# Moving two small steps of the key maximum one query product later in a linear-attention stage

## The chip, the cores and the metric

The kernel runs on one core of a Trainium2 chip. The metric is the time of one execution on the device, in microseconds (us), and a kernel's time is the median of its runs. The engines are TensorE (PE in the profile, with PEld for its weight loads), VectorE (DVE), ScalarE (ACT), GpSimd (POOL) and SyncE (SP).

## The reference

A network of two layers over 1024 nodes with 512 features: in each, a graph part, a mixing part and a feed-forward part. The change lies in the mixing part of the first, two blocks (`l` = 0, 1) of attention with random features (8 heads of 64, 256 features each):

```python
def softmax_kernel(data, proj, is_query, eps=0.0001):
    ...
    data_dash = jnp.einsum('bhnd,md->bhnm', data * normalizer, proj)
    diag = jnp.sum(data ** 2, axis=-1, keepdims=True) * 0.5 * normalizer ** 2
    if is_query:
        m = jnp.max(data_dash, axis=-1, keepdims=True)
    else:
        m = jnp.max(data_dash, axis=(-2, -1), keepdims=True)
    ...
    return ratio * (jnp.exp(data_dash - diag - m) + eps)
...
qp = softmax_kernel(q, proj[i], True)
kp = softmax_kernel(k, proj[i], False)
k_sum = kp.sum(axis=2)
d_inv = 1.0 / jnp.einsum('bhnm,bhm->bhn', qp, k_sum)
ctx = jnp.einsum('bhnm,bhnd->bhmd', kp, v)
o = jnp.einsum('bhmd,bhnm,bhn->bhnd', ctx, qp, d_inv)
```

A query row needs only the maximum of its own row before its exponential. The keys need one maximum for a whole head, over all 1024 nodes and 256 features.

## The kernel before, in words

Every engine has a program written out by hand, and semaphores tie them together. Each result of TensorE in PSUM is a job, a bank of 512 columns. There are eight banks; job n takes bank n modulo 8 and waits (`open_job`) until job n-8 has been read. `job_plan` lists the jobs in order, with the engine that frees each: A for ScalarE, D for VectorE. The order of the list must be the order in which TensorE runs them.

The attention of a block works on four pairs of heads (`hp` = 0 to 3), so there are eight pairs in the kernel. Their stretches run from about 140 to 273 us (block 0) and from 567 to 705 us (block 1). A pair goes like this:

- `kd`: eight products of 128 nodes each, keys by random features (L792, two PE instructions for each product). ScalarE copies each to `kd` (L1326), and VectorE then takes its row maxima, `kmax` (L1733).
- For pairs 1 to 3 VectorE then does two subtractions for the output of the pair before (`o_to_lo`, L1726), and after them reduces `kmax` to `kmaxp`, a column of maxima for each of the two heads (L1739).
- `qd`: eight products, queries by random features (L792 too). For each, VectorE takes the negative row maximum (L1743) and adds the diagonal term (L1745); this is the bias `nqmax`, and ScalarE then writes the exponential to `G` (`query_exp`, two instructions on L1334 for each product).
- `kt`: TensorE transposes `kmaxp` (L798), VectorE reduces the two rows to two numbers, `kneg` (L1749), and sets them on a diagonal, `kdiag` (L1751).
- `kb`: TensorE spreads the two numbers to all partitions, `ones` by `kdiag` (L803), and VectorE copies them to `nkmax` (L1755). With `nkmax` as bias ScalarE takes the exponential of the keys in place in `kd`, one instruction for each head (L1341), and counts `kexp_done` after each.
- `ctx`: 64 PE instructions, keys by values (L819). They wait for `kexp_done`: the first half for the first head's exponential, the second half for the second's. It follows the eighth query product on TensorE.
- `eT` turns `G` (L810), `o` multiplies by the context (L833), and VectorE divides.

GpSimd runs beside this: it issues the indirect DMAs that add edges to two tables (L2348), and between them makes the low parts of weights, a pass of about 5 us over 128x2048 elements (`lo`, L2273), when its own list comes to them. In block 1 it has no wait for the attention in its list.

The steps `kt` and `kb` are put inside the loop over the query products: on TensorE after product `t`, on VectorE after the two `nqmax` instructions of product `t`, and on ScalarE the exponentials of the keys come after a number of `query_exp`.

Of the kernel before, what the change touches and what calls it, by code (L numbers as in the profile page):

```python
# [32 lines left out]
D = 512  # L33
NT = N // P
# [65 lines left out]
def job_plan():  # L100

    stages = [("xn_T", 8, "AD"), ("gnn_w_T", 4, "AD"), ("par_T", 1, "D"), ("hg", 4, "A"), ("y_T0", 8, "AD"), ("hg", 4, "A"),
              ("edge_T", 1, "D"), ("proj0", 1, "A")]
    for l in range(DEPTH):
        if l:
            stages += [(f"q{l}", 2, "A"), (f"y_T{l}", 4, "AD"), (f"q{l}", 6, "A")]
        else:
            stages.append((f"q{l}", 8, "A"))  # L110
        stages += [(f"k{l}", 1, "A"), (f"rq{l}", 2, "A"), (f"k{l}", 2, "A"), (f"dq{l}", 1, "A"), (f"k{l}", 5, "A"),
                   (f"v{l}", 1, "D"), (f"rk{l}", 2, "A"), (f"v{l}", 1, "D"), (f"dk{l}", 1, "A"), (f"v{l}", 6, "D"), (f"vsum{l}", 1, "A")]
        for hp in range(HEADS // 2):
            s = f"{l}.{hp}"
            stages += [("kd" + s, 8, "AD"), ("qd" + s, 2, "A"), ("kt" + s, 1, "D"), ("qd" + s, 2, "A"),
                       ("kb" + s, 1, "D"), ("qd" + s, 4, "A"), ("ctx" + s, 1, "D"), ("eT" + s, 8, "D"),
                       ("o" + s, 4, "D")]
        stages += [(f"wo{l}", 6, "D"), (f"y2_T{l}", 4, "AD"), (f"wo{l}", 2, "D"),
                   (f"up{l}.0", 2, "A"), (f"y2_T{l}", 4, "AD"), (f"up{l}.0", 6, "A"), (f"down{l}.0", 8, "D")]
        for fb in range(1, MLP):  # L120
            stages.append((f"up{l}.{fb}", 8, "A"))
            if fb + 1 < MLP or l + 1 == DEPTH:
                stages.append((f"down{l}.{fb}", 8, "D"))
            else:
                stages += [(f"proj{l + 1}", 1, "A"), (f"down{l}.{fb}", 6, "D"), (f"y_T{l + 1}", 4, "AD"), (f"down{l}.{fb}", 2, "D")]
    stages += [("gnn", 6, "D"), ("xt_T", 4, "AD"), ("gnn", 2, "D"), ("gate_T", 1, "A"), ("xt_T", 4, "AD"), ("gate_T", 1, "A"), ("gate", 1, "D"),
               ("deg", 1, "D"), ("rank", 1, "D"),
               ("xT0", visit_tiles(0), "AD")]
    for v in range(VISITS):
        n = visit_tiles(v)  # L130
        stages.append((f"g0.{v}", n, "A"))
        if v:
            stages.append((f"hT{v - 1}", 2 * visit_tiles(v - 1), "AD"))
        stages.append((f"u0.{v}", n, "D"))
        if v:
            stages.append((f"down_e{v - 1}", visit_tiles(v - 1), "A"))
        stages.append((f"g1.{v}", n, "A"))
        if v + 1 < VISITS:
            stages.append((f"xT{v + 1}", visit_tiles(v + 1), "AD"))
        stages.append((f"u1.{v}", n, "D"))  # L140
    stages += [(f"hT{VISITS - 1}", 2 * visit_tiles(VISITS - 1), "AD"), (f"down_e{VISITS - 1}", visit_tiles(VISITS - 1), "A")]
    stages += [("wv_T", 4, "AD"), ("wth_T", 4, "AD"), ("x3_T", 8, "AD"), ("gram", 4, "AD"), ("gwv", 4, "AD"),
               ("kv", 4, "AD"), ("mean", 1, "A"), ("fc_T", 4, "AD"), ("xkv", 8, "D"), ("h", 8, "D"), ("h_T", 4, "AD"),
               ("w0_T", 1, "A"), ("w1_T", 2, "AD"), ("agg0", 2, "D"), ("h_T", 4, "AD")]
    for g in range(2):
        stages += [(f"agg{g}", 8 if g else 6, "D"), (f"f_T{g}", 8, "AD"), (f"rst{g}", 6 if g else 8, "D")]
    stages += [("u_T", 2, "D"), ("rst1", 2, "D")]
    for i in range(STEPS + 2):
        if i == 2:
            stages.append(("u_T", 2, "D"))  # L150
        if i == STEPS:
            stages.append(("alu_T", 1, "D"))
        if i < STEPS:
            stages.append((f"alu_in{i}", 3, "A"))
        if 0 < i <= STEPS:
            stages.append((f"alu_mid{i - 1}", 3, "A"))
        if i > 1:
            stages.append((f"alu_out{i - 2}", 1, "D"))
    stages.append(("alu_T", 1, "D"))
    first, place, seen, who, acts, dones = {}, {}, {}, [], [], []  # L160
    for name, count, engines in stages:
        first.setdefault(name, len(who))
        for _ in range(count):
            place[name, seen.get(name, 0)] = len(who)
            seen[name] = seen.get(name, 0) + 1
            who.append(engines)
            acts.append((acts[-1] if acts else 0) + ("A" in engines))
            dones.append((dones[-1] if dones else 0) + ("D" in engines))
    return first, place, who, acts, dones
# [15 lines left out]
def gps_network(nc, a, out):  # L185
# [67 lines left out]
    with ExitStack() as ctx:  # L253
# [26 lines left out]
        kd = place("kd", [P, 2, NT, NBF], F32, at_b)  # L280
# [342 lines left out]
        def _(pe):  # L623
# [136 lines left out]
            for l in range(DEPTH):  # L760
# [25 lines left out]
                for hp in range(HEADS // 2):  # L786
                    s = f"{l}.{hp}"
                    for x, feat in (("kd", k_T), ("qd", q_T)):
                        for t in range(NT):
                            n = JOB_AT[x + s, t]  # L790
                            open_job(n)
                            pe.matmul(bank(n), feat[:, hp, t * P:(t + 1) * P], proj[:, :, :].rearrange("p a m -> p (a m)"),  # L792
                                      start=True, stop=True).then_inc(job_full, 1)
                            if x == "qd" and t == 1:
                                n = JOB["kt" + s]
                                open_job(n)
                                pe.wait_ge(kmax_ready, 4 * l + hp + 1)
                                pe.transpose(bank(n)[0:2, 0:P], kmaxp[:, :], ident[:, :]).then_inc(job_full, 1)  # L798
                            if x == "qd" and t == 3:
                                n = JOB["kb" + s]  # L800
                                open_job(n)
                                pe.wait_ge(kdiag_ready, 4 * l + hp + 1)
                                pe.matmul(bank(n)[:, 0:2], ones[0:2, :], kdiag[:, :], start=True, stop=True).then_inc(job_full, 1)  # L803
# [365 lines left out]
        def _(act):  # L1169
# [113 lines left out]
            for l in range(DEPTH):  # L1283
# [37 lines left out]
                for hp in range(HEADS // 2):  # L1321
                    s = f"{l}.{hp}"
                    for t in range(NT):
                        n = JOB["kd" + s] + t
                        act.wait_ge(job_full, n + 1)
                        act.activation(kd[:, :, t, :], bank(n).rearrange("p (h m) -> p h m", h=2), ACT.Copy).then_inc(job_act, 1)  # L1326
                        if hp and t == 3:
                            o_to_hi(hp - 1)

                    def query_exp(t):  # L1330
                        n = JOB_AT["qd" + s, t]
                        act.wait_ge(qbias_ready, NT * (4 * l + hp) + t + 1)
                        for h in range(2):
                            ins = act.activation(G[:, t, h * NBF:(h + 1) * NBF], bank(n)[:, h * NBF:(h + 1) * NBF], ACT.Exp, bias=nqmax[:, t, h:h + 1])  # L1334
                        ins.then_inc(job_act, 1)

                    for t in range(2):
                        query_exp(t)
                    act.wait_ge(job_done, DONES[JOB["kb" + s]])
                    for h in range(2):  # L1340
                        act.activation(kd[:, h, :, :], kd[:, h, :, :], ACT.Exp, bias=nkmax[:, h:h + 1]).then_inc(kexp_done, 1)  # L1341
                    for t in range(2, NT):
                        query_exp(t)
                o_to_hi(HEADS // 2 - 1)
                split_hi(f"down{l}.0")
# [213 lines left out]
        def _(dve):  # L1559
# [121 lines left out]
            for l in range(DEPTH):  # L1681
# [46 lines left out]
                for hp in range(HEADS // 2):  # L1728
# [11 lines left out]
                    for t in range(NT):  # L1740
# [2 lines left out]
                        link(dve.tensor_reduce(nqmax[:, t, :], bank(n).rearrange("p (h m) -> p h m", h=2), AX_X, ALU.max,  # L1743
                                               negate=True))
                        dve.tensor_tensor(nqmax[:, t, :], nqmax[:, t, :], dexp[:, 0, t, 2 * hp:2 * hp + 2], ALU.add).then_inc(qbias_ready, 1)  # L1745
                        if t == 1:
                            n = JOB["kt" + s]
                            dve.wait_ge(job_full, n + 1)
                            dve.tensor_reduce(kneg[:, :], bank(n)[0:2, 0:P], AX_X, ALU.max, negate=True).then_inc(job_done, 1)  # L1749
                            dve.wait_ge(job_done, DONES[n])  # L1750
                            dve.tensor_scalar(kdiag[:, :], ident[0:2, 0:2], kneg[:, :], None, ALU.mult).then_inc(kdiag_ready, 1)  # L1751
                        if t == 3:
                            n = JOB["kb" + s]
                            dve.wait_ge(job_full, n + 1)
                            dve.tensor_copy(nkmax[:, :], bank(n)[:, 0:2]).then_inc(job_done, 1)  # L1755
# [736 lines left out]
```

## Time and profile before

| | |
|---|---|
| median of 3 runs | 1825.57 us (1815.61, 1825.57, 1827.23) |
| profiled execution | 1821.88 us |
| its span, first to last instruction | 1819.8 us |
| mean granted TensorE clock | 0.969 |
| busy PE, DVE, ACT, POOL | 92%, 61%, 37%, 55% |

The profile is of one execution, which took 2.08 us more than the span of its instructions. Times are from the start of the span. A timeline row gives start, duration, engine, line, operation, output<-inputs, how many instructions were merged, and in brackets how long the engine was idle before and what released it. The ends of matmuls are modelled: of merged matmuls each starts about 0.43 us after the one before, while the row's duration runs on to the modelled end of the last.

### The profile page before, as it was taken

The page shows a single profiled execution, that of the slowest core. Times are in us where ns is not written, and L with a number is a line of the kernel's source. Part 1 is how long each engine was busy: PE and PEld are TensorE (multiplying, and loading weights), DVE is VectorE, ACT ScalarE, POOL GpSimd, SP SyncE. Part 2 cuts the span into 40 slices and gives each one's busy share as a digit, 9 for nine tenths or more (in the row PEclk, how much of TensorE's full clock was granted, in tenths as well). Part 3 has the DMA queues.
Part 4 walks back from the last instruction along what each step waited for, and adds up shares of the span by engine and source line. Part 5 has one row for each costly group of instructions (what it writes and reads, how often), then busy time and mean ns, then how long its engine had stood idle before and what let it go on. Part 6 is the DMA issues. An engine that isn't in the chain of part 4 may idle for free.

```text
span 1819.8 us, 19994 instructions
## 1 busy us (share of the span) xinstructions
PE 1679.2 (92%) x7799; PEld 1304.6 (72%) x7799; DVE 1102.6 (61%) x1845; ACT 675.7 (37%) x880; POOL 999.0 (55%) x534
## 2 busy tenths in 40 slices
PE   5989999999899989999996899999999489999987
PEld 4765558788776547788885778778787478887863
DVE  6697778999877887643257433333423475432385
ACT  3324535232424344332312565655555221211112
POOL 3336802466778888588722676666677452333312
PEclk9999999999999999999997999999999799999987
DMA  9363202455342222332243877777775501121001
GB/s 334 109 194 55 24 1 61 116 116 117 64 82 1 24 24 1 83 57 47 70 156 128 310 248 262 247 266 260 250 266 180 190 15 54 63 70 58 12 1 46
DMA packets 146509, 212.05 MB, mean 117 GB/s; under 512 B 43725, under 2 KB 60337, under 8 KB 145169
## 3 DMA queue, kind: packets, MB, share of 16 engines
q1 hardware_dynamic: 98464, 176.96, 29.7%
q0 software_dynamic: 42832, 18.84, 8.3%
q10 hardware_dynamic: 5120, 14.99, 2.5%
q8 instruction: 62, 1.02, 0.2%
q14 instruction: 31, 0.25, 0.0%
HBM read 186.69 MB, written 30.08 MB: 119 GB/s over the span
## 4 chain that ended last, share of the span: by engine, by line
PE 76%; DVE 16%; ACT 3%; issue 3%; POOL 1%; DMA 1%; SPq 0%; DVEq 0%; POOLq 0%
PE PS L643 20%; PE PS L645 20%; PE PS L644 20%; PE PS L792 4%; PE PS L819 3%; PE PS L833 3%; PE PS L810 2%; POOL slots_x L2386 1%; DVE op_b L1613 1%; PE PS L686 1%; DVE kmax L1733 1%; DVE h_op L1995 1%; ACT W L1423 1%; DVE picked L1636 1%; DVE X L2037 1%
## 5 line engine op out<-in xcount | busy, mean ns | idle before, releaser
L2273 POOL TENSOR_TENSOR W<-raw,W 128x2048 fp32r<-128x2048 f32 x40 | 193.3, 4834 | 289.8 <-ACT W L1189 289.8
L2348 POOL DMA_INDIRECT table_w<-edge_add,edge_ix x128 | 205.9, 1609 | 109.7 <-DMA table_w<-edge_add,edge_ix 59.9
L2348 POOL DMA_INDIRECT table_c<-edge_add,edge_ix x128 | 208.0, 1625 | 73.2 <-DMA table_c<-edge_add,edge_ix 39.4
L643 PE MATMUL PS<-op_b,W 128*128 128x512 f32 x576 | 226.8, 394 | 7.2 <-DVE op_b L1613 4.6
L644 PE MATMUL PS<-op_b,W 128*128 128x512 f32 x576 | 225.5, 391 | 0.0
L645 PE MATMUL PS<-op_b,W 128*128 128x512 f32 x576 | 225.2, 391 | 0.0
L643 PE MATMUL PS<-W,op_a 128*128 128x512 f32 x480 | 188.7, 393 | 3.3 <-DVE op_a L1801 1.8
L645 PE MATMUL PS<-W,op_a 128*128 128x512 f32 x480 | 187.6, 391 | 0.0
L644 PE MATMUL PS<-W,op_a 128*128 128x512 f32 x480 | 187.4, 390 | 0.0
L2391 POOL TENSOR_TENSOR W<-raw,W 128x2048 fp32r<-128x2048 f32 x30 | 143.3, 4790 | 44.4 <-ACT W L1423 44.4
L1189 ACT ACTIVATE W<-raw 128x2048 fp32r<-128x2048 f32 x40 | 76.5, 1920 | 162.2 <-PE PS L645 105.1
L643 PEld LDWEIGHTS PS<-op_b,W 128*128 128x128 f32 x576 | 108.9, 189 | 32.2 <-DVE op_b L1613 4.0
L645 PEld LDWEIGHTS PS<-op_b,W 128*128 128x128 f32 x576 | 108.9, 189 | 23.0
L644 PEld LDWEIGHTS PS<-op_b,W 128*128 128x128 f32 x576 | 108.9, 189 | 22.3
L1357 ACT ACTIVATE G<-PS,colv 128x512 f32<-128x512 f32 x64 | 44.3, 691 | 179.4 <-PE PS L645 179.4
L643 PEld LDWEIGHTS PS<-W,op_a 128*128 128x128 f32 x480 | 90.7, 189 | 23.8 <-issue 3.2
L643 PE MATMUL PS<-W,x_op 128*128 128x512 f32 x248 | 98.7, 398 | 6.2 <-DVE x_op L1985 4.8
L645 PEld LDWEIGHTS PS<-W,op_a 128*128 128x128 f32 x480 | 90.5, 189 | 19.1
L644 PEld LDWEIGHTS PS<-W,op_a 128*128 128x128 f32 x480 | 90.7, 189 | 18.7
L1985 DVE TENSOR_TENSOR x_op<-PS,x_op 128x512 fp32r<-128x512 f32 x21 | 13.9, 688 | 145.0 <-ACT x_op L1430 145.0
L1801 DVE TENSOR_TENSOR op_a<-G,op_a 128x512 fp32r<-128x512 f32 x64 | 63.0, 1006 | 58.4 <-ACT op_a L1358 58.1
L1423 ACT ACTIVATE W<-raw 128x2048 fp32r<-128x2048 f32 x46 | 87.9, 1914 | 25.7 <-DMA raw<-in_L_ffn_w_dram 15.7
(427 smaller groups left out, 3794.1 us busy)
## 6 DMA issues: line engine op xcount, KB each, us to landing
raw<-in_L_ffn_w_dram SPq DMA_DIRECT2D x46, 1024.0 KB, 5.7
raw_e<-in_L_ffn_w_dram SPq DMA_DIRECT2D x22, 1024.0 KB, 6.1
raw_v<-in_L_ffn_w_dram SPq DMA_DIRECT2D x22, 1024.0 KB, 5.2
raw<-in_L_mix_W_dram SPq DMA_DIRECT2D x16, 1024.0 KB, 5.5
raw<-table_c SPq DMA_DIRECT2D x10, 1024.0 KB, 5.1
key_row<-key_dram SPq DMA_DIRECT2D x32, 256.0 KB, 4.0
w_row<-in_edge_weight_dram SPq DMA_DIRECT2D x32, 256.0 KB, 5.2
table_w<-zero POOLq DMA_DIRECT2D x4, 1024.0 KB, 7.9
```

The source lines that it names most:

```text
L643: pe.matmul(ps, lhs_hi, rhs_hi, start=start, stop=False)
L644: pe.matmul(ps, lhs_hi, rhs_lo, start=False, stop=False)
L645: return pe.matmul(ps, lhs_lo, rhs_hi, start=False, stop=stop)
L792: pe.matmul(bank(n), feat[:, hp, t * P:(t + 1) * P], proj[:, :, :].rearrange("p a m -> p (a m)"), start=True, stop=True).then_inc(job_full, 1)
L819: mm = pe.matmul(bank(n)[:, (2 * h + mh) * VW:(2 * h + mh + 1) * VW], kd[:, h, t, mh * P:(mh + 1) * P], V[:, t, 2 * hp + h, :], start=(t = ...
L833: mm = pe.matmul(bank(n)[h * DH:(h + 1) * DH, :], ctx_sb[:, part, 2 * h + mh, :], E_T[:, 2 * h + mh, c * HALF:(c + 1) * HALF], start=(mh = ...
L1189: act.activation(W[:, s % SLOTS, 0, :], raw[:, raw_no[name] % 2, :], ACT.Copy).then_inc(hi_done, 1)
L1423: act.activation(ring_w[b % RING][:, 0, :], ring_raw[b % RING], ACT.Copy).then_inc(block_hi, 1)
L1801: dve.tensor_tensor(op_a[:, 1, at], G[:, j, :], op_a[:, 0, at].bitcast(F32), ALU.subtract).then_inc(hidden, 1)
L2273: pool.tensor_tensor(lo_at, raw[:, r % 2, :], hi_at.bitcast(F32), ALU.subtract).then_inc(lo_done, 1)
L2348: pool.indirect_dma_start(out=tb, out_offset=bass.IndirectOffsetOnAxis(ap=edge_ix[:, i, c:c + 1].bitcast(U32), axis=0), in_=edge_add[:, i, ...
L2391: pool.tensor_tensor(ring_w[b % RING][:, 1, :], ring_raw[b % RING], ring_w[b % RING][:, 0, :].bitcast(F32), ALU.subtract)\
```

## The change

On all three engines the transpose of the key maxima (`kt`) stands behind the third query product in place of the second, and the spreading product (`kb`) behind the fifth in place of the fourth. ScalarE does three query exponentials before those of the keys, in place of two. Nothing is added and nothing removed.

```diff
-            stages += [("kd" + s, 8, "AD"), ("qd" + s, 2, "A"), ("kt" + s, 1, "D"), ("qd" + s, 2, "A"),
-                       ("kb" + s, 1, "D"), ("qd" + s, 4, "A"), ("ctx" + s, 1, "D"), ("eT" + s, 8, "D"),
+            stages += [("kd" + s, 8, "AD"), ("qd" + s, 3, "A"), ("kt" + s, 1, "D"), ("qd" + s, 2, "A"),
+                       ("kb" + s, 1, "D"), ("qd" + s, 3, "A"), ("ctx" + s, 1, "D"), ("eT" + s, 8, "D"),
...
-                            if x == "qd" and t == 1:
+                            if x == "qd" and t == 2:
                                 n = JOB["kt" + s]
...
-                            if x == "qd" and t == 3:
+                            if x == "qd" and t == 4:
                                 n = JOB["kb" + s]
...
-                    for t in range(2):
+                    for t in range(3):
                         query_exp(t)
                     act.wait_ge(job_done, DONES[JOB["kb" + s]])
                     for h in range(2):
                         act.activation(kd[:, h, :, :], kd[:, h, :, :], ACT.Exp, bias=nkmax[:, h:h + 1]).then_inc(kexp_done, 1)
-                    for t in range(2, NT):
+                    for t in range(3, NT):
                         query_exp(t)
...
-                        if t == 1:
+                        if t == 2:
                             n = JOB["kt" + s]
...
-                        if t == 3:
+                        if t == 4:
                             n = JOB["kb" + s]
```

On VectorE, in the first pair of block 0 (the others alike), these instructions stood between the bias of the second query product and the copy of the spread maxima, before the change:

```order
L1743 TENSOR_REDUCE nqmax<-PS 128x2
L1745 TENSOR_TENSOR nqmax<-nqmax,dexp 128x2
L1749 TENSOR_REDUCE kneg<-PS 2x1
L1751 TENSOR_SCALAR kdiag<-ident,kneg 2x2
L1743 TENSOR_REDUCE nqmax<-PS 128x2
L1745 TENSOR_TENSOR nqmax<-nqmax,dexp 128x2
L1743 TENSOR_REDUCE nqmax<-PS 128x2
L1745 TENSOR_TENSOR nqmax<-nqmax,dexp 128x2
L1755 COPY nkmax<-PS 128x2
```

And these after it, from the bias of the second product too:

```order
L1743 TENSOR_REDUCE nqmax<-PS 128x2
L1745 TENSOR_TENSOR nqmax<-nqmax,dexp 128x2
L1743 TENSOR_REDUCE nqmax<-PS 128x2
L1745 TENSOR_TENSOR nqmax<-nqmax,dexp 128x2
L1749 TENSOR_REDUCE kneg<-PS 2x1
L1751 TENSOR_SCALAR kdiag<-ident,kneg 2x2
L1743 TENSOR_REDUCE nqmax<-PS 128x2
L1745 TENSOR_TENSOR nqmax<-nqmax,dexp 128x2
L1743 TENSOR_REDUCE nqmax<-PS 128x2
L1745 TENSOR_TENSOR nqmax<-nqmax,dexp 128x2
L1755 COPY nkmax<-PS 128x2
```

The instructions are the same, but five biases and no longer four (counted from the first product) stand ahead of `nkmax`, and three and no longer two ahead of `kneg`.

On TensorE, in the same pair:

```order
 L792 MATMUL PS<-proj,k_T 128x512 x8
-L792 MATMUL PS<-proj,q_T 128x512 x2
+L792 MATMUL PS<-proj,q_T 128x512 x3
 L798 MATMUL PS<-ident,kmaxp 2x128
 L792 MATMUL PS<-proj,q_T 128x512 x2
 L803 MATMUL PS<-kdiag,ones 128x2
-L792 MATMUL PS<-proj,q_T 128x512 x4
+L792 MATMUL PS<-proj,q_T 128x512 x3
 L819 MATMUL PS<-V,kd 128x65 x32
```

Here a row counts products as the program writes them, which the profile shows as two PE instructions each. One query product moved from behind `kb` to ahead of `kt`; the two between them stay two.

## Rows read from the trace of the kernel before

**Rows 1.** The page, chain that ended last: share of the span by engine.

```profile
PE 76%; DVE 16%; ACT 3%; issue 3%; POOL 1%; DMA 1%; SPq 0%; DVEq 0%; POOLq 0%
```

**Rows 2.** Waits of PE, whole span: total us, times, longest.

```profile
PE PS L798 <- DVE kmaxp L1739: 10.3, 6, 5.0
```

**Rows 3.** Timeline of PE, second pair of block 0.

```profile
180.44 1.45 PE L792 MATMUL PS<-proj,q_T 128*128 128x512 f32 x3
182.96 0.27 PE L798 MATMUL PS<-ident,kmaxp 128*2 128x128 f32 x1 [1.07 <-DVE kmaxp L1739]
183.07 1.88 PE L792 MATMUL PS<-proj,q_T 128*128 128x512 f32 x4
184.99 0.35 PE L803 MATMUL PS<-kdiag,ones 2*128 2x2 f32 x2
185.27 3.70 PE L792 MATMUL PS<-proj,q_T 128*128 128x512 f32 x8
188.81 1.45 PE L819 MATMUL PS<-V,kd 128*128 128x65 f32 x12
```

**Rows 4.** Timeline of DVE, the same pair.

```profile
181.45 1.28 DVE L1726 TENSOR_TENSOR op_a<-o_mul,op_a 128x512 fp32r<-128x512 f32 x2
182.65 0.16 DVE L1739 TENSOR_REDUCE kmaxp<-kmax 128x2 f32<-128x16 f32 x1
182.73 0.68 DVE L1743 TENSOR_REDUCE nqmax<-PS 128x2 f32<-128x512 f32 x1
...
183.53 0.68 DVE L1743 TENSOR_REDUCE nqmax<-PS 128x2 f32<-128x512 f32 x1
...
184.32 0.27 DVE L1749 TENSOR_REDUCE kneg<-PS 2x1 f32<-2x128 f32 x1
184.63 0.22 DVE L1751 TENSOR_SCALAR kdiag<-ident,kneg 2x2 f32<-2x2 f32 x1
...
186.35 0.15 DVE L1755 COPY nkmax<-PS 128x2 f32<-128x2 f32 x1
```

**Rows 5.** Timelines of ACT and of PE's weight loads, the same pair.

```profile
186.53 3.90 ACT L1341 ACTIVATE kd<-kd,nkmax 128x2048 f32<-128x2048 f32 x2 [1.25 <-DVE nkmax L1755]
...
188.44 1.99 ACT L1341 ACTIVATE kd<-kd,nkmax 128x2048 f32<-128x2048 f32 x1
...
188.65 2.48 PEld L819 LDWEIGHTS PS<-V,kd 128*128 128x128 f32 x21 [0.51 <-issue]
```

**Rows 6.** Timelines of DVE and PE, first pair of block 0.

```profile
152.88 0.15 DVE L1755 COPY nkmax<-PS 128x2 f32<-128x2 f32 x1
...
155.34 1.90 PE L819 MATMUL PS<-V,kd 128*128 128x65 f32 x16
```

**Rows 7.** Windows of two pairs: PE, PEld, DVE, ACT, POOL busy; PEclk, DMA share, GB/s.

```profile
173.00:206.50 33.50, 32.39 (x165) 19.04 (x163) 26.64 (x47) 15.47 (x28) 26.40 (x17) 1.00 0.23 7
...
632.80:671.70 38.90, 33.92 (x165) 19.55 (x163) 30.63 (x47) 15.47 (x28) 31.28 (x19) 0.96 0.27 28
```

**Rows 8.** Timelines of POOL, DVE and PE, third pair of block 1.

```profile
640.16 5.09 POOL L2273 TENSOR_TENSOR W<-raw,W 128x2048 fp32r<-128x2048 f32 x1
...
641.21 5.20 DVE L1726 TENSOR_TENSOR op_a<-o_mul,op_a 128x512 fp32r<-128x512 f32 x2
...
650.91 0.15 DVE L1755 COPY nkmax<-PS 128x2 f32<-128x2 f32 x1
...
646.63 0.27 PE L798 MATMUL PS<-ident,kmaxp 128*2 128x128 f32 x1 [4.98 <-DVE kmaxp L1739]
646.74 3.33 PE L792 MATMUL PS<-proj,q_T 128*128 128x512 f32 x4
...
650.50 3.70 PE L792 MATMUL PS<-proj,q_T 128*128 128x512 f32 x8
654.04 7.25 PE L819 MATMUL PS<-V,kd 128*128 128x65 f32 x64
```

**Rows 9.** Timeline of POOL at the start of block 1.

```profile
497.74 4.68 POOL L2273 TENSOR_TENSOR W<-raw,W 128x2048 fp32r<-128x2048 f32 x1 [0.75 <-ACT W L1189]
```

## Prediction

> **What bounds the kernel now.** I read the chain that ended last first: TensorE carries 76% of it and VectorE 16% [rows 1]. So a wait of TensorE counts unless it is given back. The list of its waits then shows one that the change bears on: the transpose of the key maxima waited for `kmaxp` six times, 10.3 us in all, the longest 5.0 us [rows 2]. Five of the six are 1.07 us each, as in [rows 3]; the sixth, of 4.98 us, is in the third pair of block 1 [rows 8]. The first pair of each block has none, since no subtractions stand ahead of `kmaxp` there. That list tells what is idle, not what is late. For that I read one pair engine by engine in order of time.
>
> In the second pair of block 0 TensorE issues its second query product until 181.89 and is idle to 182.96 [rows 3]. VectorE meanwhile has no gap: subtractions, `kmaxp` at 182.65, two biases, `kneg` at 184.32, `kdiag` at 184.63, two more biases, `nkmax` at 186.35, all back to back [rows 4]. ScalarE starts the keys' exponential at 186.53, 0.18 us after `nkmax` starts, and the first head's takes 1.99 us, so it ends at 188.52. The weight load of `ctx` starts 0.13 us later, at 188.65, after an unusual gap of 0.51 us [rows 5], and the first `ctx` matmul at 188.81. The last of the eight query matmuls before it, started at 185.27, gives way at about 185.27 + 8 x 0.43 = 188.71 [rows 3]. So in this pair `ctx` waits for the exponential of the keys, by only 0.1 us; the chain that sets its start is `kmaxp`, four biases, `kneg`, `kdiag`, `nkmax` on VectorE and then ScalarE, not TensorE. The other handover is as tight: `kdiag` ends at 184.85 and the spreading product starts at 184.99, 0.14 us later, while TensorE could have come at 183.07 + 4 x 0.43 = 184.79.
>
> **The change part by part.**
>
> *The query product ahead of the transpose* fills 2 x 0.43 = 0.86 us of the 1.07 us of idle time. It makes `kmaxp` no earlier: that waits for VectorE's subtractions. `kt` still starts at 182.96, and 0.21 us of the wait is left. The product it fills the gap with needs a free bank, that of the third or fourth key product, whose maximum VectorE took long before; so the gap is truly filled. Taken alone this is worth 0.86 us in each pair with a wait.
>
> *The transpose behind the third bias on VectorE* puts one more pair of instructions (L1743, L1745) ahead of `kneg`. Two such pairs start at 182.73 and 183.53 [rows 4], so one costs 0.80 us. `kneg` moves from 184.32 to 185.12, `kdiag` ends at 185.65, and the spreading product starts at 185.79. TensorE comes to it at 184.79 as before (the two products between `kt` and `kb` stay two), so it now waits 1.00 us there, where it waited 0.20. The 0.86 is nearly gone: three products are left behind `kb` and not four, so TensorE comes to `ctx` at 185.79 + 0.28 + 6 x 0.43 = 188.65, against 188.71.
>
> *The spreading product behind the fifth bias* keeps two biases between `kdiag` and `nkmax`, so `nkmax` starts at 186.35 + 0.80 = 187.15; the spread value is there by then. The third query exponential on ScalarE, moved ahead of the keys', needs the third bias, ready at 185.1, and takes about 0.8 us: done by 186.0, hidden. The keys' exponential starts at 187.33, its first half ends at 189.32, and `ctx` starts at 189.45 (load) and 189.61 (matmul): **0.80 us later than before**. The second half is wanted 32 matmuls later and has slack. What follows `ctx` shifts with it: the transposes of `G` wait for query exponentials, of which five and not six now follow the keys' exponential on ScalarE, so they end at the same time as before and are still early. The bank of the third query product, which `ctx` itself now waits for, is free by 186.0.
>
> The first pair of each block has no wait to fill, yet the same chain: `nkmax` at 152.88, `ctx` at 155.34 [rows 6], the same 2.46 us as in the second pair (186.35 to 188.81). It also loses 0.80.
>
> *Sum for block 0:* four pairs x 0.80 = +3.20 us. What comes between the blocks is bound by TensorE and shifts with it. GpSimd too: at the start of block 1 its pass waited 0.75 us for ScalarE [rows 9], and ScalarE follows TensorE, so GpSimd's list starts block 1 as much later as TensorE does.
>
> *Block 1, pairs one and two:* +1.60. But in the third pair VectorE's two subtractions took 5.20 us and not 1.28 [rows 8, 4]: they started 1.05 us into a pass of GpSimd of 5.09 us and ended about when it did. GpSimd's list holds no wait for the attention here, so the pass does not move by these 1.60 us. If the subtractions come 1.60 us later into the same pass, they end at the same time, and the 1.60 is **taken back**: 3.92 us of delay become 2.32. The page "SBUF — State Buffer" of the Trainium skill (section "Who interferes with whom") says that a VectorE instruction with two inputs in SBUF and a GpSimd instruction that reads SBUF exclude each other, and the one that comes second is blocked for the whole of the first; by that rule the 1.60 is taken back. Were the 5.20 us instead a length of the subtractions themselves, nothing would be, and the sum below would be 1.60 higher; I go by the ends that the rows show to coincide, and keep the higher value in the range.
>
> *Block 1, third pair:* after the idle 4.98 us TensorE's clock is low for a while (four matmuls took 3.33 us where 1.88 is normal; 0.96 granted over this pair against 1.00 in the second pair of block 0 [rows 7]). Here the fourth bias waited for its product, so `nkmax` at 650.91 hangs on the second product behind `kt`, and there are two products between `kt` and `kb` in both kernels: `nkmax` stays. The exponential then ends at 650.91 + 0.18 + 1.99 = 653.08. TensorE, with three products and not four to do from 650.50, comes to `ctx` at 653.08 too; so `ctx` starts at about 653.3 and not 654.04: -0.75.
>
> *Block 1, fourth pair:* +0.80. Later stages are tied to TensorE's or VectorE's own work and shift along.
>
> **Sum:** 3.20 + 1.60 - 1.60 - 0.75 + 0.80 = **+3.25 us**. The profiled execution took 1821.88 us, so it would give 1825.1; the median shown is 1825.57, which would give 1828.8. The one and the other differ by the spread of the runs (11.6 us); I take the middle, **1827 us**. By the bounds: all eight pairs at +0.80 and nothing taken back is +6.4; nothing below by this mechanism. A difference within 1% (18 us) is about what a measurement of this kernel cannot tell from no change.
>
> **The rivals.**
>
> *A: TensorE is the bound, and the filled wait stays filled.* Six pairs x 0.86 = -5.2 us: 1818 to 1820. For it: the 76% of the chain and the 10.3 us of waits. Against: both handovers, at `kb` and at `ctx`, are within 0.2 us of being late already. It would need some 0.8 us of slack in VectorE's chain, which shows none. Chance 0.12.
>
> *B: an even trade.* TensorE waits at `kb` for what it saved at `kt`, but the keys' exponential has slack after all (the 0.1 us at `ctx` is then the modelled end of the matmuls). Each pair gives 188.65 - 188.71 = -0.06; with the -0.75 of the third pair of block 1, about -1: 1823. Chance 0.15.
>
> *C: slower than now by over 1%: the clock.* A pair would hold three idle stretches within 7 us (0.21 at `kt`, 1.00 at `kb`, 0.9 at `ctx`) where it has had about 1.4 us. The granted clock stayed 1.00 in a pair with the single gap of 1.07 [rows 7], and fell to its lower level, 1.2 in place of 2.4 GHz, after the gap of 4.98. Each fall costs 3.33 - 1.88 = 1.45 us or more. If it fell in all eight pairs: 6.4 + 8 x 1.45 = +18 us, 1842 to 1844. The point that decides is whether TensorE's idle time in a pair, now 2.1 us in pieces, acts like 5 us in one; nothing in the trace says so. Chance 0.03.
>
> *D: the collision with GpSimd moves.* If GpSimd's pass falls clear of the subtractions, as a shift of some 3 us between the two engines' lists could bring, 3.92 + 1.45 us go: about 1822. If it adds a second collision, +5.4: 1832. Chance 0.08, half each.
>
> **How the numbers follow.** The forecast (a loss of 0.5 to 1 us in nearly every pair, +2 to +6.4 in all) has 0.62; A 0.12, B 0.15, C 0.03, D 0.08. The range of 1818 to 1836 holds the forecast with its +6.4 and a few us of the spread of runs to either side, B and D; A lies on its lower edge. Over 1% faster would need 18 us, more than all waits at `kt` together: 0.02. Over 1% slower is C and little else: 0.04. Within 1%: 0.94.
>
> **What the profile would show.** At `kt` a wait of about 0.2 us in four pairs of the five of 1.07, at `kb` about 1.0 us where it had 0.2, from `kmaxp` to `nkmax` 4.50 us where it was 3.70, from `nkmax` to `ctx` 2.46 as before, so 6.96 from `kmaxp` to `ctx` in place of 6.16. TensorE's pair goes from 33.5 to 34.3 us. Wrong it would be if `nkmax` came earlier than that, which would mean that VectorE did not run its list back to back, or if `ctx` did not follow `nkmax`.

## The result, and the profile after

The changed kernel takes 1829.45 us (median of 20 runs), the one before 1822.62 us (20 runs): the ratio is 1.0034, with a 95% interval of 1.0023 to 1.0044, or 4.2 to 8.0 us more. That is within 1%, but clear of the noise of 20 runs. The profiled execution has a span of 1825.4 us, 5.6 us more than that of before.

The page has the chain that ended last moved a little from TensorE to the engines that it waits for [rows 1]:

```profile
PE 74%; DVE 17%; ACT 4%; issue 3%; POOL 1%; DMA 1%; SPq 0%; DVEq 0%; POOLq 0%
```

In the waits of PE over the whole span, the wait that the query product was to fill went from 10.3 to 4.8 us [rows 2]:

```profile
PE PS L798 <- DVE kmaxp L1739: 4.8, 6, 3.8
```

The timeline of PE over the second pair of block 0 shows what came in its place [rows 3]:

```profile
181.10 2.74 PE L792 MATMUL PS<-proj,q_T 128*128 128x512 f32 x6
184.05 0.27 PE L798 MATMUL PS<-ident,kmaxp 128*2 128x128 f32 x1 [0.21 <-DVE kmaxp L1739]
184.16 1.88 PE L792 MATMUL PS<-proj,q_T 128*128 128x512 f32 x4
186.88 0.35 PE L803 MATMUL PS<-kdiag,ones 2*128 2x2 f32 x2 [0.84 <-DVE kneg L1749]
187.16 2.84 PE L792 MATMUL PS<-proj,q_T 128*128 128x512 f32 x6
190.57 7.33 PE L819 MATMUL PS<-V,kd 128*128 128x65 f32 x64 [0.57 <-issue]
```

One idle stretch of 1.07 us has become three: 0.21 at the transpose, 0.84 at the spreading product, 0.57 ahead of `ctx`. VectorE's and ScalarE's timelines of the same pair say why [rows 4, 5]:

```profile
183.74 0.16 DVE L1739 TENSOR_REDUCE kmaxp<-kmax 128x2 f32<-128x16 f32 x1
...
185.41 0.68 DVE L1743 TENSOR_REDUCE nqmax<-PS 128x2 f32<-128x512 f32 x1
...
186.20 0.27 DVE L1749 TENSOR_REDUCE kneg<-PS 2x1 f32<-2x128 f32 x1
186.51 0.22 DVE L1751 TENSOR_SCALAR kdiag<-ident,kneg 2x2 f32<-2x2 f32 x1
...
188.23 0.15 DVE L1755 COPY nkmax<-PS 128x2 f32<-128x2 f32 x1
...
188.42 3.90 ACT L1341 ACTIVATE kd<-kd,nkmax 128x2048 f32<-128x2048 f32 x2 [1.26 <-DVE nkmax L1755]
```

The third bias, at 185.41, stands ahead of `kneg`. From `kmaxp` to `nkmax` it is 4.49 us, where it was 3.70; from `nkmax` to `ctx` 2.34, where it was 2.46; so `ctx` comes 6.83 us behind `kmaxp`, where it was 6.16. Its 64 matmuls then take 7.16 us to the first transpose of `G`, where they took 7.09. The pair, from its first key product to that of the next, takes 208.34 - 174.13 = 34.21 us and took 206.51 - 173.04 = 33.47: **0.74 us more**. The pairs without a disturbance are alike: seven of eight have 6.82 to 6.91 us from `kmaxp` to `ctx`. Before, the same seven had 6.16, but for the first pair of block 1 with 6.42.

The eighth is the third pair of block 1, where GpSimd's pass meets the subtractions [rows 8]. Timelines of POOL, DVE and PE there:

```profile
645.32 5.09 POOL L2273 TENSOR_TENSOR W<-raw,W 128x2048 fp32r<-128x2048 f32 x1
...
646.71 4.86 DVE L1726 TENSOR_TENSOR op_a<-o_mul,op_a 128x512 fp32r<-128x512 f32 x2
...
651.80 0.37 PE L798 MATMUL PS<-ident,kmaxp 128*2 128x128 f32 x1 [3.79 <-DVE kmaxp L1739]
651.96 3.62 PE L792 MATMUL PS<-proj,q_T 128*128 128x512 f32 x4
655.51 0.58 PE L803 MATMUL PS<-kdiag,ones 2*128 2x2 f32 x2
656.03 3.41 PE L792 MATMUL PS<-proj,q_T 128*128 128x512 f32 x6
659.28 7.25 PE L819 MATMUL PS<-V,kd 128*128 128x65 f32 x64
```

The windows of these two pairs (PE, PEld, DVE, ACT, POOL busy; PEclk, DMA share, GB/s) give the granted clock [rows 7]:

```profile
174.13:208.34 34.21, 32.59 (x165) 18.98 (x163) 26.54 (x47) 15.54 (x28) 26.59 (x17) 1.00 0.24 8
638.29:676.98 38.69, 34.90 (x166) 20.08 (x164) 30.29 (x47) 15.53 (x28) 30.70 (x19) 0.91 0.27 28
```

The pass itself came 5.16 us later than before (640.16 to 645.32), nearly as late as the subtractions (5.50). The subtractions began 1.39 us into it, and 1.05 before, so only 0.34 us was taken back. In both kernels they ended 1.16 us behind the end of the pass. The clock was low over more of the pair (0.91, and 0.96 before): six query matmuls behind `kb` took 3.41 us, where six take 2.84 at the high clock. From the transpose to `ctx` it was 7.48 us, and 7.41 before.

### The profile page after: what moved, and what is told of

Read it like the earlier page. It is cut to its first block, busy times and chain, and to the rows that moved or that the text cites. A ratio compares the mean times of both kernels' runs of the same rounds, so it can differ in the third digit from the quotient of the medians.

```text
span 1825.4 us, 19994 instructions
## 1 busy us (share of the span) xinstructions
PE 1679.3 (92%) x7799; PEld 1302.1 (71%) x7799; DVE 1103.7 (60%) x1845; ACT 676.1 (37%) x880; POOL 1000.7 (55%) x534
## 4 chain that ended last, share of the span: by engine, by line
PE 74%; DVE 17%; ACT 4%; issue 3%; POOL 1%; DMA 1%; SPq 0%; DVEq 0%; POOLq 0%
PE PS L643 20%; PE PS L644 20%; PE PS L645 20%; PE PS L819 3%; PE PS L833 3%; PE PS L792 3%; PE PS L810 2%; POOL slots_x L2386 1%; DVE nqmax L1743 1%; DVE op_b L1613 1%; PE PS L686 1%; DVE kmax L1733 1%; DVE h_op L1995 1%; ACT W L1423 1%; DVE picked L1636 1%
## 5 line engine op out<-in xcount | busy, mean ns | idle before, releaser
L1189 ACT ACTIVATE W<-raw 128x2048 fp32r<-128x2048 f32 x40 | 76.5, 1920 | 161.6 <-PE PS L645 104.8
L1801 DVE TENSOR_TENSOR op_a<-G,op_a 128x512 fp32r<-128x512 f32 x64 | 63.0, 1006 | 58.2 <-ACT op_a L1358 57.7
```

The lines of the kernel that those rows point to most:

```text
L1189: act.activation(W[:, s % SLOTS, 0, :], raw[:, raw_no[name] % 2, :], ACT.Copy).then_inc(hi_done, 1)
L1801: dve.tensor_tensor(op_a[:, 1, at], G[:, j, :], op_a[:, 0, at].bitcast(F32), ALU.subtract).then_inc(hidden, 1)
```

## The experiments

Two places were to be told apart: VectorE's list up to `nkmax`, and TensorE's wait at `kb`. Ratios are against the kernel before, on the same chip. The cuts of code for e1 to e4 show only the order in `job_plan`, drawn together on one line; the loops of TensorE and VectorE follow it. ScalarE does three query exponentials ahead of those of the keys in e1, two in e2 and e3, four in e4.

**One part alone.** In e1 only `kt` moves:

```diff
-("qd" + s, 2, "A"), ("kt" + s, 1, "D"), ("qd" + s, 2, "A"), ("kb" + s, 1, "D"), ("qd" + s, 4, "A")
+("qd" + s, 3, "A"), ("kt" + s, 1, "D"), ("qd" + s, 1, "A"), ("kb" + s, 1, "D"), ("qd" + s, 4, "A")
```

> Only the transpose kt moves (behind the third query product, with three query exponentials ahead of the keys'); the spreading product kb stays behind the fourth. Theory 1, the loss comes from the number of biases ahead of nkmax on VectorE: that number stays at four, so nkmax stays 3.70 us behind kmaxp, ctx 6.16 us behind kmaxp, a pair at 33.5 us, and the time equals the kernel before's within 1 us. Theory 2, the loss comes from TensorE's new wait at kb (kneg stands behind a third bias here too, and TensorE comes to kb 0.86 us after kt's next product): each pair loses some 0.7 us, +5 to +6 us in all, as with the full change. Theory 3, TensorE is the bound and the filled wait pays: -5 us.

Measured: 1829.16 us, ratio 1.0027 (1.0009 to 1.0045). Theory 1 expected no change, and was wrong here; what theory 2 expected came about. Timelines of PE and DVE, second pair of block 0:

```profile
182.87 0.27 PE L798 MATMUL PS<-ident,kmaxp 128*2 128x128 f32 x1 [0.21 <-DVE kmaxp L1739]
182.98 1.02 PE L792 MATMUL PS<-proj,q_T 128*128 128x512 f32 x2
185.70 0.35 PE L803 MATMUL PS<-kdiag,ones 2*128 2x2 f32 x2 [1.70 <-DVE kdiag L1751]
185.98 3.70 PE L792 MATMUL PS<-proj,q_T 128*128 128x512 f32 x8
189.51 2.68 PE L819 MATMUL PS<-V,kd 128*128 128x65 f32 x23
...
182.56 0.16 DVE L1739 TENSOR_REDUCE kmaxp<-kmax 128x2 f32<-128x16 f32 x1
...
186.25 0.15 DVE L1755 COPY nkmax<-PS 128x2 f32<-128x2 f32 x1
```

`nkmax` is where it was, 3.69 us behind `kmaxp`. But `kdiag` is late, TensorE waits 1.70 us at `kb`, and four products still stand behind it: `ctx` follows the last of them, 6.95 us behind `kmaxp`. So two paths lead from `kmaxp` to `ctx`, one over VectorE and ScalarE, one over TensorE's wait at `kb` and the products behind it, and each makes `ctx` late by itself. In two of the six pairs with the wait of 1.70 us (the second and third of block 1) the clock fell too: the eight query matmuls behind it took 5.40 us in place of 3.70, and `ctx` came 8.6 us behind `kmaxp`.

In e2 only `kb` moves:

```diff
-("qd" + s, 2, "A"), ("kt" + s, 1, "D"), ("qd" + s, 2, "A"), ("kb" + s, 1, "D"), ("qd" + s, 4, "A")
+("qd" + s, 2, "A"), ("kt" + s, 1, "D"), ("qd" + s, 3, "A"), ("kb" + s, 1, "D"), ("qd" + s, 3, "A")
```

> Only the spreading product kb moves (behind the fifth query product); the transpose kt stays behind the second, and ScalarE keeps two query exponentials ahead of the keys'. Theory 1 (number of biases ahead of nkmax): five stand there, so nkmax is 0.80 us later behind kmaxp (4.50), ctx 6.83 behind kmaxp as in the changed kernel, a pair 34.2 us, +5 to +6 us in all; kt's wait stays at 1.07 us, kb has none. Theory 2 (TensorE's wait at kb): that wait is gone here, so no loss, within 1 us of before.

Measured: 1829.43 us, ratio 1.0022 (1.0007 to 1.0037). Timelines of PE and DVE, fourth pair of block 0:

```profile
260.27 0.38 PE L803 MATMUL PS<-kdiag,ones 2*128 2x2 f32 x2
260.58 2.84 PE L792 MATMUL PS<-proj,q_T 128*128 128x512 f32 x6
264.01 2.19 PE L819 MATMUL PS<-V,kd 128*128 128x65 f32 x18 [0.59 <-ACT kd L1341]
...
257.19 0.16 DVE L1739 TENSOR_REDUCE kmaxp<-kmax 128x2 f32<-128x16 f32 x1
...
261.68 0.15 DVE L1755 COPY nkmax<-PS 128x2 f32<-128x2 f32 x1
```

There is no wait at `kb`, and the loss is there all the same: `nkmax` 4.49 us behind `kmaxp`, `ctx` 6.82, as in the changed kernel, and TensorE idle on ScalarE. So in the full change, where `kb` also has three products behind it, VectorE's list sets `ctx`, and theory 2 does not explain the loss there. The time of e2 holds more than this, though: in its trace the clock fell over the `ctx` matmuls of two pairs (see e4).

**The other way, and twice as far.** e3 and e4 set the two steps behind products 1 and 3, and behind 4 and 6:

```diff
-("qd" + s, 2, "A"), ("kt" + s, 1, "D"), ("qd" + s, 2, "A"), ("kb" + s, 1, "D"), ("qd" + s, 4, "A")
+("qd" + s, 1, "A"), ("kt" + s, 1, "D"), ("qd" + s, 2, "A"), ("kb" + s, 1, "D"), ("qd" + s, 5, "A")
```

> The other way: kt behind the first query product, kb behind the third. Theory 1: nkmax comes 0.80 us earlier behind kmaxp (2.90), but in pairs two to four TensorE waits 0.86 us longer at kt (1.93) and has five products behind kb, so that ctx follows the eighth product and no longer the exponential: ctx 0.66 to 0.8 us later behind kmaxp than before (6.8 to 7.0), some 0.7 us in each of six pairs, +4 to +5 us; the first pair of each block, without a wait at kt, changes little. So the place before would be the balance between the two chains. If VectorE's chain alone set the time, it would be -6 us.

Measured: 1829.94 us, ratio 1.0030 (1.0015 to 1.0044), as theory 1 has it. Timeline of PE, third pair of block 0:

```profile
218.88 0.27 PE L798 MATMUL PS<-ident,kmaxp 128*2 128x128 f32 x1 [1.93 <-DVE kmaxp L1739]
...
221.11 4.56 PE L792 MATMUL PS<-proj,q_T 128*128 128x512 f32 x10
225.51 1.67 PE L819 MATMUL PS<-V,kd 128*128 128x65 f32 x14
```

`nkmax` came 3.13 us behind `kmaxp`, but `ctx` 6.93 (218.58 to 225.51), with no idle time ahead of it: TensorE's own five products hold it. Seven pairs have 6.93 or 6.94 (the eighth, which meets GpSimd's pass, 8.34), also the first of each block, for which I had expected little change: it waits 0.85 us at `kt` now. The place before is the balance of the two paths.

```diff
-("qd" + s, 2, "A"), ("kt" + s, 1, "D"), ("qd" + s, 2, "A"), ("kb" + s, 1, "D"), ("qd" + s, 4, "A")
+("qd" + s, 4, "A"), ("kt" + s, 1, "D"), ("qd" + s, 2, "A"), ("kb" + s, 1, "D"), ("qd" + s, 2, "A")
```

> Double dose: kt behind the fourth query product and kb behind the sixth, four query exponentials ahead of the keys'. Theory 1: two biases more ahead of nkmax than before, 5.30 us from kmaxp to nkmax, ctx 7.6 us behind kmaxp, 1.5 us a pair and +12 us in all (no wait left at kt, since 1.72 us of products fill 1.07). A theory in which the loss is one disturbed place (a bank, or GpSimd's pass) gives no more than the +6 of the single dose. The clock could fall in the pairs if idle time adds up: then well over +12.

Measured: 1855.05 us, ratio 1.0178 (1.0143 to 1.0213): +32 us at the ratio, and not 12. Timeline of PE in the third pair of block 0, and windows of that pair and of the second pair of block 1:

```profile
229.41 0.35 PE L803 MATMUL PS<-kdiag,ones 2*128 2x2 f32 x2 [1.15 <-DVE kdiag L1751]
229.69 1.98 PE L792 MATMUL PS<-proj,q_T 128*128 128x512 f32 x4
233.10 12.12 PE L819 MATMUL PS<-V,kd 128*128 128x65 f32 x62 [1.42 <-ACT kd L1341]
```

```profile
215.87:257.41 41.54, 38.97 (x165) 25.58 (x164) 26.81 (x47) 15.60 (x28) 9.45 (x6) 0.84 0.08 4
629.32:664.32 35.00, 32.43 (x166) 19.04 (x164) 26.28 (x47) 15.60 (x28) 29.00 (x19) 1.00 0.22 1
```

The list counts as expected: `kmaxp` to `ctx` is 7.62 us in all eight pairs, 1.46 us more than before, 11.7 us in all. The rest is mainly the clock. In four of the eight pairs it fell to 1.2 GHz over the `ctx` matmuls (0.50 granted from 236 to 245 us), and such a pair takes up to 41.5 us in place of 35.0. This is rival C of the prediction, at twice the dose. The idle time ahead of it does not decide by itself: with waits of 1.15 and 1.42 us the clock fell in one pair of four, with 1.42 alone in one of two, with 1.44 and 1.13 and with 1.49 and 1.08 in both. At the single dose (waits of 0.84 and 0.57) no pair of the changed kernel's trace has it. In e2's trace two of the five undisturbed pairs that wait 1.07 us at `kt` do: their waits at `ctx` are 0.67 and 0.59, those of the other three 0.58 to 0.64, and their `ctx` matmuls take 11.51 and 11.40 us.

**Without the collision.** The pass of GpSimd is put earlier in its list, to a place where VectorE reads PSUM or takes reciprocals:

```diff
                     lo(name)
                     if l:
-                        scatter(12)
+                        scatter(16 if hp else 8)
```

> The kernel before, with GpSimd's pass for the second weight of block 1 put after 8 edge columns in place of 12 (16 in place of 12 behind it), so that it falls some 15 us earlier, where VectorE reads PSUM or takes reciprocals. If the 5.20 us of the two subtractions in the third pair of block 1 came from that pass, they take 1.28 us here, the wait at kt falls from 4.98 to 1.07, the clock stays high there, and the time falls by 3.92 + about 1.45 = 5 us. If the subtractions are long for another reason, nothing changes.

> The changed kernel with the same early pass. Against e5 it shows the change without the collision: theory 1 gives eight pairs x 0.74 = 5.9 us, +0.32%. The prediction's idea that the collision takes back part of the delay, and that the third pair of block 1 gains, says that this difference is larger than that between the changed kernel and the one before, by 1.6 + 1.5 = 3 us; if GpSimd's pass simply moves with the rest or falls by chance, the two differences are alike (about 6).

Measured: e5 1820.27 us, ratio 0.9980 (0.9966 to 0.9995); e6, with the change, 1819.60, ratio 0.9982 (0.9967 to 0.9998). The collision is gone from e5's attention: the third pair of block 1 has 1.28 us of subtractions and a wait of 1.07 us at `kt`, and e5 is faster than the kernel before, as expected. But e6 is hardly slower than e5 (1.6 us in the mean, standard error 1.4), and neither theory had that. Both were run again:

> The kernel of e5 again, beside e10, because twelve runs each left the difference of e5 and e6 open: their means lie 1.6 us apart with an uncertainty of about 1.4, while their traces show each of the eight pairs 0.74 us longer with the change (5.9). If the trace's eight pairs are the whole effect, e10 less e9 is 4 to 7 us, and the four sets of runs together give some 4 us; if something behind the attention gives most of it back, the difference stays under 2 us.

> The kernel of e6 again, on the chip of e9. See there: 4 to 7 us over e9 if the eight pairs are the whole effect, under 2 us if it is given back.

Measured: e9 1819.41 us, ratio 0.9963 (0.9948 to 0.9978); e10 1819.45, ratio 0.9978 (0.9962 to 0.9993). The means of all 24 runs of either lie 0.8 us apart, with a standard error of 0.9. Yet the traces show the loss where it was foreseen: e6's first seven pairs take 5.4 us more than e5's (from the first key product of the first pair to that of the last, 530.56 and 525.18), with `ctx` 6.81 to 6.87 us behind `kmaxp` in all eight. (In e10 `ctx` is as late in each pair, but the stretch is only 2.8 us longer than e9's, whose first pair and the part between the blocks took longer than e5's.) The loss is given back later, in the feed-forward part of block 1. The list of waits of PE from 600 to 960 us, first of e5, then of e6:

```profile
PE PS L643 <- DVE op_a L1801: 5.7, 1, 5.7
```

```profile
PE PS L643 <- DVE op_a L1801: 1.6, 1, 1.6
```

Timelines of POOL, DVE, SyncE's queue and ACT ahead of that wait in e5:

```profile
741.65 5.20 POOL L2273 TENSOR_TENSOR W<-raw,W 128x2048 fp32r<-128x2048 f32 x1
...
738.49 2.28 DVE L1807 TENSOR_TENSOR X<-X,raw 128x2048 f32<-128x2048 f32 x1
...
747.28 0.51 SPq L537 DMA_DIRECT2D raw<-in_L_mix_W_dram  x1
...
755.04 1.92 ACT L1189 ACTIVATE W<-raw 128x2048 fp32r<-128x2048 f32 x1 [17.19 <-DMA raw<-in_L_mix_W_dram]
```

And of DVE, SyncE's queue and ACT in e6, where POOL's pass started at 740.26:

```profile
739.90 7.93 DVE L1801 TENSOR_TENSOR op_a<-G,op_a 128x512 fp32r<-128x512 f32 x4
747.75 2.28 DVE L1807 TENSOR_TENSOR X<-X,raw 128x2048 f32<-128x2048 f32 x1
...
750.06 0.37 SPq L537 DMA_DIRECT2D raw<-in_L_mix_W_dram  x1
...
755.31 1.92 ACT L1189 ACTIVATE W<-raw 128x2048 fp32r<-128x2048 f32 x1 [13.02 <-DMA raw<-in_L_mix_W_dram]
```

ScalarE's next weight split (L1189) waits for a load, and the activations are queued behind that split. Two things hold the load. SyncE's list has a load of `x` ahead of it, into the buffer that GpSimd's pass frees, and its own buffer is freed by VectorE's addition (L1807). In e5 the pass came last: it ended at 746.85, both loads followed, and the split started 8.2 us behind it. In e6 the addition came last: it ended at 750.03, since the subtractions ahead of it (L1801) met the pass and took 7.93 us (2.48 in the kernel before), and the split started 5.3 us behind it. So GpSimd's list bounds e5, VectorE's e6, and the two splits fall 0.3 us apart. TensorE, 4.4 us ahead in e5 at the last `ctx` matmul (688.6 and 693.0), went on at 763.98 in e5 and at 764.34 in e6. What the attention saves beyond GpSimd's list, TensorE waits for. Behind the longer wait the clock is low too (0.54 granted from 764 to 770 us in e5, 1.00 in e6). In e9 and e10 it is alike: waits of 6.0 + 1.3 us, and of 1.4 us, the split bound by the pass in e9 and by the addition in e10.

**The subtractions out of the way.** `kmaxp` waits for the subtractions of the pair before; e7 does them behind the biases:

```diff
-                    if hp:
-                        for c in range(2):
-                            o_to_lo(hp - 1, c)
                     dve.wait_ge(job_done, DONES[JOB["kd" + s] + 7])
...
+                    if hp:
+                        for c in range(2):
+                            o_to_lo(hp - 1, c)
```

> The kernel before, with the two subtractions for the pair before (L1726) moved from ahead of kmaxp to behind all eight biases. kmaxp comes 1.20 us earlier in pairs two to four, the wait at kt of 1.07 goes, ctx follows about 1.1 us earlier: five pairs x 1.07 and in the third pair of block 1 the 4.98 + 1.45, together -11 to -12 us, if the change's idle time at kt has its cause in those subtractions. If GpSimd's pass then meets the biases' additions (L1745, two inputs in SBUF) in their place, the third pair of block 1 gains nothing: -6.

Measured: 1817.12 us, ratio 0.9962 (0.9945 to 0.9979), some 7 us faster than before, as expected for the case that the pass meets the additions. Undisturbed pairs take 32.4 us, with no wait at `kt`, `kb` or `ctx`. In the third pair of block 1 the pass met a bias addition instead (on line 1742 here). Timelines of POOL, DVE and PE:

```profile
638.03 5.09 POOL L2273 TENSOR_TENSOR W<-raw,W 128x2048 fp32r<-128x2048 f32 x1
...
638.19 4.96 DVE L1742 TENSOR_TENSOR nqmax<-nqmax,dexp 128x2 f32<-128x2 f32 x1
...
644.53 0.55 PE L803 MATMUL PS<-kdiag,ones 2*128 2x2 f32 x2 [4.84 <-DVE kdiag L1748]
```

An addition over 128x2 elements, 0.16 us elsewhere, took 4.96 us.

> The changed kernel (kt behind the third product, kb behind the fifth) with the subtractions behind the biases. Against e7, theory 1: kmaxp to nkmax is 0.80 longer here too, ctx 0.7 later, +5 to +6 us in eight pairs, though TensorE has no wait at kt in either. So the loss would not hang on the wait that the change was to fill. If the loss needs that wait, e8 equals e7.

Measured: 1817.70 us, ratio 0.9971 (0.9951 to 0.9992). In its trace `ctx` comes 6.83 us behind `kmaxp` in the undisturbed pairs, with 0.4 to 0.6 us of idle time ahead of it, against 6.16 and none in e7: the loss in a pair doesn't hang on the wait that the change was to fill. (The last pair has 6.90 and 6.24.) In the time it can't be told from nothing (the means are 2.3 us apart, standard error 2.0).

> e7 (the subtractions behind the biases) and e5 (the early pass) together. e7's trace shows the pass meeting a bias addition in its third pair of block 1 and TensorE idle for 4.84 us at kb. With the pass out of the way all eight pairs should have no wait at kt, kb or ctx, 32.4 us a pair: against the kernel before six pairs x 1.07 and the 3.9 us and the low clock of the collision, -11 to -12 us, 1812 to 1813, the fastest of all. If the clock or a new meeting takes it back, no better than e7 (-7).

> e11 with the change on top (kt behind the third product, kb behind the fifth). TensorE is busy throughout in e11, so the change can only delay: kmaxp to ctx 6.83 in place of 6.16 in all eight pairs, +5 to +6 us over e11. It is the third clean measurement of the change; if the effect of the change hung on the wait at kt, it would be 0.

Measured: e11 1818.66 us, ratio 0.9960 (0.9945 to 0.9976); e12 1820.30, ratio 0.9973 (0.9956 to 0.9989). All eight pairs of e11 have 6.16 or 6.17 us from `kmaxp` to `ctx` and no idle time at the three places. Its attention is the shortest of all (from the first pair's first key product to the last pair's 520.6 us, before 531.0), but the time is that of e7 and not 1812 to 1813: TensorE waits 5.9 + 1.3 us in the feed-forward part of block 1, as in e9. In e12 the same stretch takes 526.1 us, 5.5 more; its times are higher by 2.4 us in the mean (standard error 1.6).

## Why the prediction was right, and which of its terms were not

*The sign and the mechanism were right.* One more bias ahead of `nkmax` on VectorE's list made `ctx` later in every undisturbed pair. The predicted handovers came: 0.21 us at `kt` (in all five pairs that had 1.07, where the prediction has four), a new wait at `kb`, `kmaxp` to `nkmax` 4.50 (measured 4.49). The time, 1829.45, lies in the range; the predicted +3.25 us was low, since the ratio gives 4.2 to 8.0 us. That 1827 comes as near as it does is in part luck: it started from 1823.7 us for the kernel before, whose median over 20 runs is 1822.62.

*The size per pair was near.* 0.80 us were foretold, 0.74 measured. The `ctx` handover was put at 2.46 us behind `nkmax` as before, and is 2.34. So the prediction read one step of the kernel before wrongly, by 0.12 us: `ctx` waited there not for the exponential of the keys, but for TensorE's own last product, on the path over `kdiag`, `kb` and the four products behind it. Both paths lead through VectorE's `kneg` and `kdiag` and were even to 0.12 us. `ctx` is 0.67 us later behind `kmaxp` for it, and its matmuls take the other 0.07. The wait at `kb` is 0.84 by the row and 1.00 in the prediction, for the row counts from the modelled end of the matmuls.

*The term that failed is the one that took 1.60 us back* in the third pair of block 1. It rested on GpSimd's pass moving by the delay of block 0 alone. The list started 3.19 us later, as predicted (497.74 to 500.93), but a longer first pass (5.10 us, before 4.68) and its own DMA waits brought the pass to 5.16 us later, and 0.34 us was taken back. That VectorE's two-input instruction waits for a pass already begun held: the subtractions ended 1.16 us behind the pass in five traces (before, after, e1, e2, e3), wherever they had started. In e1 they started 3.62 us into the pass and took 2.65 us; so a delay can be taken back as the prediction has it, if the pass doesn't move along. In e7 a bias addition ended with the pass.

*The term of -0.75 us* for the same pair failed as well: it took the low clock to last as before, and it lasted over more of the pair. From `kt` to `ctx` +0.07 us was measured. Without these two terms the sum would have been eight times the pair's, 8 x 0.74 = 5.9 us, which is what the ratio shows.

*The rivals.* A (the filled wait pays) is refuted: `ctx` came later behind `kmaxp` in each pair. B (the exponential of the keys has slack) is refuted by e2, where no wait at `kb` stands beside its delay. C, the clock, is not seen in the change's trace, but it is real: e4 has it in four of eight pairs, e2 and e1 in two each. D, the collision, stayed where it was.

*What the prediction did not have* is the second path through `kb` (it was worked out for the full change and then dropped, which made e1's expectation wrong), and GpSimd's list as a bound on the feed-forward part of block 1. The latter is shown in the traces of e5 and e6, and of e9 and e10. How much of the attention's loss reaches the end of the kernel differs between the four kernels that the change was put into, and the split at about 755 us shows where, with what its load waited for last:

| without and with the change | split starts | last wait of the load | difference of means, us (standard error) |
|---|---|---|---|
| before, after | 755.79, 761.63 | addition, addition | 6.1 (0.9) |
| e5, e6 | 755.04, 755.31 | pass, addition | 1.6 (1.4) |
| e9, e10 | 762.11, 760.06 | pass, addition | 0.0 (1.2) |
| e7, e8 | 752.85, 756.57 | addition, addition | 2.3 (2.0) |
| e11, e12 | 751.02, 755.82 | pass, pass | 2.4 (1.6) |

Where VectorE's addition holds the load in both, the attention's delay passes on (5.84 and 3.72 us). Where GpSimd's pass holds it without the change, the loss is hidden until the addition comes later than the pass. In e11 and e12 the pass itself moved by 4.82 us. These are single traces, and GpSimd's list varies by several us from trace to trace (the pass stands at 741.65 in e5 and at 748.61 in e9, the same kernel), so the table shows a way by which the means can differ, and does not prove it for them.

## What to carry to other kernels

A wait of the bounding engine is worth filling only if what it waits for is not itself the way to the next wait. Follow each step from the waited-for value to the next place where the engine waits, by every path: here two paths were even to 0.1 us, so that moving a small step by one product, either way, or either step alone, cost 0.7 to 0.8 us a pair. The gain lay in the list of the engine that was waited for: what could stand behind the urgent step (the subtractions of the pair before) stood ahead of it, and moving it paid 7 us. An engine with a list of its own pace, such as GpSimd's here, can take back what is saved.

## What was not expected of the hardware

- TensorE's clock fell behind waits that other pairs of the same trace had without a fall: 1.15 and 1.42 us in e4 (one pair of four), 1.07 and about 0.6 us in e2 (two of five), 0.21 and 1.70 us or more in e1 (two of six). In e4 and e2 `ctx` then took 11.4 to 12.4 us in place of 7.3. Waits of 1.93 us in the five undisturbed pairs of e3 that have them, and of 0.84 and 0.57 us in the changed kernel, were not followed by it. What decides is open.
- One VectorE addition over 128x2 elements took 4.96 us in place of 0.16 when it started 0.16 us into a pass of GpSimd of 5.09 us (e7), and 4.55 us when it started 0.57 us into one (e8).
